# Attention with relative positions on one core: the trip of a score tile through device memory in four column quarters instead of two halves

## What is computed

```
def _relative_shift(x):
    b, h, s, _ = x.shape
    x = jnp.pad(x, ((0, 0), (0, 0), (0, 0), (1, 0)))
    x = x.reshape(b, h, s + 1, s)
    return x[:, :, 1:, :].reshape(b, h, s, s)
...
content_score = jnp.einsum('bhsp,bhtp->bhst', q + u, k)
pos_score = jnp.einsum('bhsp,htp->bhst', q + v, pos)
pos_score = _relative_shift(pos_score)
score = (content_score + pos_score) / jnp.sqrt(jnp.float32(P))
weights = jax.nn.softmax(score, axis=-1)
out = jnp.einsum('bhst,bhtp->bhsp', weights, val)
```

## Time and profile before

| | us |
|---|---|
| median of 3 runs | 11101.68 |
| lowest and highest | 11082.91 and 11107.82 |
| the profiled execution | 11115.23 |
| its span in the profile | 11113.4 |
| PE, ACT, DVE, POOL busy in the span | 9422.7, 6687.5, 6258.0, 2944.3 |

### The profile page before, as it was taken

One profiled execution on the slowest core, in us unless ns is written; L12 is line 12 of the kernel. 1 busy time (PEld: TensorE's weight loads), 2 busy tenths in 40 slices (PEclk: granted clock), 3 DMA queues, 4 the chain that ended last, 5 costly groups with the idle time before them and its releaser, 6 DMA issues. The chain is left out here.

```text
span 11113.4 us, 271423 instructions
## 1 busy us (share of the span) xinstructions
PE 9422.7 (85%) x95520; PEld 6711.5 (60%) x95520; DVE 6258.0 (56%) x14730; ACT 6687.5 (60%) x11009; POOL 2944.3 (26%) x3520
## 2 busy tenths in 40 slices
PE   5888888999688888899968888889996888888999
PEld 3665665666465666566646656656663565665666
DVE  3655663765365566376446556637644565663764
ACT  3666663765466666376546666637644666663764
POOL 2333332001233333200123333310012333331001
PEclk7999999999899999999989999999998999999999
DMA  6999992000699999100069999911007999991100
GB/s 240 378 363 366 381 378 87 26 25 16 233 377 366 361 379 380 59 25 25 16 254 380 367 362 382 365 46 27 23 18 265 373 372 362 379 357 48 27 22 26
DMA packets 747623, 2482.45 MB, mean 223 GB/s; under 512 B 111745, under 2 KB 133761, under 8 KB 745921
## 3 DMA queue, kind: packets, MB, share of 16 engines
q1 hardware_dynamic: 746176, 2463.84, 60.3%
HBM read 1280.34 MB, written 1183.07 MB: 222 GB/s over the span
## 5 line engine op out<-in xcount | busy, mean ns | idle before, releaser
L658 DVE CUSTOM_DVE_ANT_0 z<-sc,z 128x1024 f32<-128x1024 f32 x2048 | 2496.5, 1220 | 1848.5 <-DMA z<-rel_rows 1608.0
L716 POOL TENSOR_SCALAR z<-z,nmax 128x1024 f32<-128x1024 f32 x2048 | 2277.8, 1123 | 4028.5 <-DVE nmax L668 4028.5
L631 ACT ACTIVATE pT<-rg 128x512 f32<-128x512 f32 x4096 | 2445.9, 598 | 738.7 <-PE rg L541 679.5
L541 PE MATMUL rg<-ident,z 128*128 128x128 f32 x16384 | 2527.0, 277 | 77.0 <-issue 68.3
L639 ACT ACTIVATE rel<-rg 128x512 f32<-128x512 f32 x3072 | 1721.1, 596 | 1407.2 <-PE rg L522 1401.8
L541 PEld LDWEIGHTS rg<-ident,z 128*128 128x128 f32 x16384 | 1990.3, 142 | 784.6 <-ACT rel L639 294.4
L522 PE MATMUL rg<-pos_s,qv_s 96*128 96x512 bf16 x4096 | 1590.8, 396 | 1021.4 <-DVE rel L693 901.6
L1013 DVE CUSTOM_DVE_ANT_0 z<-sc,mask 128x1024 f32<-128x1024 f32 (+7 forms) x1536 | 1359.1, 910 | 227.0 <-PE sc L832 173.9
L952 ACT ACTIVATE pT<-rg 128x512 f32<-128x512 f32 (+3 forms) x1792 | 928.4, 550 | 763.0 <-PE rg L885 751.0
L522 PEld LDWEIGHTS rg<-pos_s,qv_s 96*128 96x128 bf16 x4096 | 478.7, 118 | 1498.0 <-DVE rel L693 1150.9
L960 ACT ACTIVATE z<-z,nmax 128x128 f32<-128x128 f32 (+15 forms) x1024 | 1226.6, 1198 | 89.0 <-POOL nmax L978 76.7
(11 more groups left out here) (93 smaller groups left out, 8161.5 us busy)
## 6 DMA issues: line engine op xcount, KB each, us to landing
rel_rows<-rel SPq DMA_DIRECT2D x2048, 512.0 KB, 7.2
z<-rel_rows SPq DMA_DIRECT2D x2048, 512.0 KB, 7.1
xnT<-qu_parts SPq DMA_DIRECT2D x792, 64.0 KB, 2.3
xnT<-v_heads SPq DMA_DIRECT2D x132, 256.0 KB, 4.3
v_heads<-rel SPq DMA_DIRECT2D x8, 4096.0 KB, 12.5
k_sb<-k_parts SPq DMA_DIRECT2D x408, 64.0 KB, 2.3
qv_s<-qv_parts SPq DMA_DIRECT2D x384, 64.0 KB, 6.2
pos_s<-pos_parts SPq DMA_DIRECT2D x384, 64.0 KB, 7.2
```

Of the source, the lines that this page charges most:

```text
L541: mm = e.transpose(rg[:, T_BANK[q], (j - 4 * q) * P:(j - 4 * q + 1) * P], z[:, n % RING, j * P:(j + 1) * P], ident[:, :])
L631: e.activation(pT[:, t % 2, q * CH:(q + 1) * CH], rg[:, T_BANK[q], :], ACT.Exp, scale=SCALE).then_inc(p_ready[q], 1)
L658: e.tensor_tensor_reduce(out=zs, in0=scf[:, 2 * half * CH:2 * (half + 1) * CH], in1=zs, scale=1.0, scalar=-3.0e38, op0=ALU.add, op1=ALU.ma ...
L716: e.tensor_scalar(zs, zs, 1.0, nmax[:, n % 2:n % 2 + 1], ALU.mult, ALU.add).then_inc(AA[done], 1)
```

## The change

Each half becomes two quarters of 512 columns, the width of one copied block. The quarters go in the order 3, 0, 1, 2, in which the copies of a tile are made, and each write waits only for the copy of its own block. The expected count of a slot rises from 32 to 64 for each use.

```diff
@@ in_order
-                                for per in (G, G // OB, 32 * G // RING, HB // NB * QK_INC, HB // NB * 16)))
+                                for per in (G, G // OB, 64 * G // RING, HB // NB * QK_INC, HB // NB * 16)))
@@ moved
-            return base.moves + 32 * (n // RING + 1)
+            return base.moves + 64 * (n // RING + 1)
@@ sp_attn_a
-            def read_half(n, half):
-
-                k, hd, i0, c0 = n % RING, n // NT % NB, n % NT * P, half * S // 2
-                shifted = bass.AP(tensor=rel_d.tensor, offset=hd * FLAT + (i0 + 1) * S + c0, ap=[[S, P], [1, S // 2]])
-                e.dma_start(z[:, k, c0:c0 + S // 2], shifted).then_inc(rel_in[k], 16)
-
-            def write_half(base, n, half):
-
-                k, hd, i0, c0 = n % RING, n // NT % NB, n % NT * P, half * S // 2
-                for c in ((R_DVE, R_ACT[-1]) if half else (R_ACT[1],)):
-                    e.wait_ge(r_copied[c], e.snap(base.tiles + (n + 1)))
-                    settle(e)
-                there = bass.AP(tensor=rel_d.tensor, offset=hd * FLAT + i0 * (S + 1) + 1 + c0, ap=[[S + 1, P], [1, S // 2]])
-                e.dma_start(there, rel[:, k, c0:c0 + S // 2]).then_inc(rel_out[k], 16)
+            def read_chunk(n, c):
+
+                k, hd, i0, c0 = n % RING, n // NT % NB, n % NT * P, c * CH
+                shifted = bass.AP(tensor=rel_d.tensor, offset=hd * FLAT + (i0 + 1) * S + c0, ap=[[S, P], [1, CH]])
+                e.dma_start(z[:, k, c0:c0 + CH], shifted).then_inc(rel_in[k], 16)
+
+            def write_chunk(base, n, c):
+
+                k, hd, i0, c0 = n % RING, n // NT % NB, n % NT * P, c * CH
+                e.wait_ge(r_copied[c], e.snap(base.tiles + (n + 1)))
+                settle(e)
+                there = bass.AP(tensor=rel_d.tensor, offset=hd * FLAT + i0 * (S + 1) + 1 + c0, ap=[[S + 1, P], [1, CH]])
+                e.dma_start(there, rel[:, k, c0:c0 + CH]).then_inc(rel_out[k], 16)
...
-                for half in range(2):
+                for c in (R_DVE, *R_ACT):
                     if here(n):
-                        read_half(n, half)
+                        read_chunk(n, c)
                     if here(r):
-                        write_half(base, r, half)
+                        write_chunk(base, r, c)
```

## The result

| | us |
|---|---|
| median before, 4 runs | 11104.75 (11082.91 to 11111.82) |
| median after, 4 runs | 11700.88 (11698.28 to 11744.06) |
| ratio, 95% interval | 1.0549 (1.0521 to 1.0578) |
| the profiled execution after | 11744.06, span 11742.3 |

A forecast was written before the change was run, and what follows sets the result against it. Attention A was taken as bound by DMA engine throughput, 5.83 us a tile; packets 0.22 plus completions 0.03 made 6.08 us, 248 us over 1024 tiles at 97%, forecast 11,365 us, 2.2% slower. Range 11,090 to 11,900.

The forecast's parts named there:

- The bound: Attention A: throughput of the full DMA engines sets 5.83 us a tile; VectorE waits for rows read back, TensorE behind it.
- The packet term: Attention A's DMA engines: 32 more packets on each engine at a fixed 7.0 ns, 0.22 us a tile.
- the price of four more transfers a tile: Completions in attention A: four more short packets a tile on each engine at 7 ns, 0.03 us; nothing larger added.
- the cover for SP's longer program: SP's issue: four more transfers, 1.5 to 1.9 us, fit its 1.98 us of waits a tile; costed at nothing.
- The high end of the packet term: DMA engines: 16.5 ns more per two 2 KB packets, from half idle engines' 159.1 ns; 0.53 us a tile.
- the SP rival: SP becomes the limit if eight issues exceed 0.56 us each; at 0.70 us +1040 us, 12,160; chance 0.15.
- the argument against it: SP's long issues look like the engines' own rate handed back, so would halve with the transfer size.
- A faster alternation: Rival: smaller reads and writes end the engines' mutual disturbance, 0.44 us a tile; -190 us, 10,925; chance 0.11.
- The three marks: Signs in the changed kernel's steady stretch: about 6.1 us a tile, GB/s near 365, mean packet near 90 ns.
- The page's rule: Trainium skill: about 3 bus cycles a packet beside its bytes; 2.3% more, 0.13 us a tile, 11,241 us in all.

The follow-up runs named there:

- the run with packets alone: Against the kernel before: four transfers of 512 KB a tile, each of two blocks with a gap, so rows of 2 KB; 1.0213, +237 us.
- Quarters in pairs: Against the changed kernel: its eight transfers a tile in the order read, read, write, write, twice; 1.0544 to the kernel before.

## Why the prediction was right and wrong

**The bound was read rightly in its place.** Attention A, the DMA rate, VectorE's wait and TensorE's behind it took all of the loss. VectorE's and ScalarE's work a tile is as it was (3.53 and 3.95 us). TensorE's rose from 5.01 to 5.15 us at a granted clock of 0.96 of 2.4 GHz in place of 0.99; with 1.3 us a tile free it does not set the rate.

**The packet term was about right.** 0.22 us a tile, 7.0 ns for each of 32 packets, is 219 us; the kernel with these packets and the old number of transfers lost 237 (218 to 256 by its interval), 0.21 us a tile in the steady stretch, and the undisturbed packets give 9 ns. Some luck may be in the closeness: that kernel also took 0.85 us more of SP's time a tile, and 0.75 us of padding cost 104 us by itself.

**The step that failed is the price of four more transfers a tile**, 0.03 us for their short packets and nothing for the rest: "A larger one is bounded by the steady stretch: the DMA queue's share is already 101%, so no gap between transfers is open there, and I add nothing." They measured 370 us, 0.41 us a tile in the steady stretch. The short packets themselves were priced well (0.04 us). The rest was not in gaps but in the large packets, of which 4.7% were long (over twice the median) in place of 1.6%. The share counts the time in which a packet is under way, and packets were under way longer: between four and eight transfers the rate fell from 367 to 344 GB/s under a share of 1.04 both times. A full share says nothing of the time lost within packets. The same reasoning took the DMA queue as the cover for SP's longer program, and that cover is thinner than it looked: 0.75 us more of SP's time a tile, inside waits of 1.98 us, cost 104 us. How much of the change's own loss goes with its 1.85 us more of SP's time, no run gives; freeing 1.0 us of it brought nothing back.

**The bounds.** The high end of the packet term, 0.53 us a tile, came from packets in half idle engines, for another reason than the one that acted, and its top, 11,670, is still 31 us under the time measured. The range held the time by luck: the SP rival, which did not come, had stretched it to 11,900.

**The rivals.** SP did not become the limit: it had 0.76 us a tile of waits left, the DMA share did not fall, and freeing it in the changed kernel brought nothing. Its condition came close, though, and the argument against it, that long issues would halve with the size, was wrong. A faster alternation did not come either; halving the turns changed nothing with quarters. The three marks that were named (about 6.1 us a tile, 365 GB/s, 90 ns a packet) were all missed on the same side (6.43, 344, 99.6), and they fit the kernel with 2 KB rows in four transfers (6.02, 367, 94.2) well. VectorE's wait grew by 0.43 us a tile where 0.25 was named, and landing shortened from 7.2 to 6.5 us for a write.

**The page's rule.** The 3 cycles a packet of the Trainium skill (DMA: Bandwidth & Descriptors, "Why small descriptors are slow (HBM only)") would have made 2.3% and 126 us; the run with packets alone gave 237, and two undisturbed 2 KB packets take 168 ns against 159, 5.7% more, so the measured 7 ns was the better figure.

**What stays open** is why more transfers make more packets long. Shown is: the 370 us come when the same packets go in eight transfers in place of four; they lie in the long packets; and they do not come with the turns between reading and writing, nor with SP's time in the changed kernel. (The two kernels also differ in the copies that a write waits for. Quarters in pairs put these waits in another order, at the same cost.) About half of them go away when the written rows start even: 202 us of the change's loss, against 27 at four transfers. One reading is that each transfer's end waits until its writes are confirmed, and that ragged ones are confirmed later. It is not shown, and the short packets at the end of a transfer, 10.3 ns in the mean, do not speak for it; a wait that stands in no packet's time would not be seen. I do not settle it.

## What to carry to other kernels

Count transfers as well as packets: in a stage that lives on the DMA rate, splitting transfers cost more than the price of smaller rows, here 0.09 us for each further transfer (0.05 with even starts). It is no price list: going down to two transfers of 1 MB with 4 KB rows gave nothing back and cost 87 us. A kernel that changes only the row length at an equal number of transfers (two pieces with a gap) takes the two apart in one run. And read the rate in GB/s beside the DMA share: a full share with a falling rate is lost time. Moving small, regular loads to another queue gained 87 us in the kernel before and lost 78 in the changed one, so it has to be tried.

## What the runs showed of the hardware that I had not expected

- With 0.75 us of padding a tile on SP the DMA share was still 1.01 (1.02 before), and the rate fell from 379 to 372 GB/s.
- More than half of the 2 KB packets took 84 ns, in every kernel that had them by the thousand; the change's further loss was in the 4.7% (1.6% with half the transfers) that took over 168 ns.
- Packets of 8 KB were worse than packets of 4 KB in the same transfers: 355 against 374 GB/s.
- A transfer over 64 partitions took SP at least 0.45 us to issue, one over 128 partitions of the same bytes 0.31 us; a read in two blocks a row took 0.52 us at least.
- Two transfers of 1 KB a tile cost 193 to 202 us in SP's queue and 66 us in GpSimd's.
